# A token tower on one core: the score stacks of batch 0 turned on TensorE from token-major parts, x of batch 1 in other tiles, the next restack in two halves

## The reference

```python
h = onehot(x) @ embeddings                      # a gather of rows
q, k, v = split(layernorm(h) @ w_qkv)           # rotary embedding on q and k
attn = softmax(q @ k.T * hd ** -0.5)
h = h + (attn @ v) @ w_proj
y = layernorm(h)
e = argmax(y @ gate_w.T)                        # one of 8 experts for each token
out = h + y + y @ expert_w[e].T
```

## Time and profile before

| | |
|---|---|
| median of the runs | 322.32 us (320.94 to 324.34) |
| profiled execution | 324.0 us |
| its span, first to last instruction | 322.2 us |
| mean granted clock of TensorE | 0.944 |
| TensorE busy | 280.8 us, 87% |
| TensorE weight loads | 201.1 us, 62% |
| VectorE busy | 243.8 us, 76% |
| ScalarE busy | 127.0 us, 39% |
| GpSimd busy | 85.7 us, 27% |

### The profile page before, as it was taken

How to read it: one execution, slowest core, us unless ns; L and a number is a source line. 1 busy time by engine, 2 the same in 40 slices (tenths; PEclk the granted TensorE clock), 3 DMA queues, 4 the chain that set the end, 5 groups by cost and what they waited for, 6 DMA issues and landing times.

```text
span 322.2 us, 5465 instructions
## 1 busy us (share of the span) xinstructions
PE 280.8 (87%) x2000; PEld 201.1 (62%) x2000; DVE 243.8 (76%) x595; ACT 127.0 (39%) x261; POOL 85.7 (27%) x96
## 2 busy tenths in 40 slices
PE   0388489888878999989998999999999999999894
PEld 0267367454655777667765776676766766667582
DVE  6766667667798879887997799687988974657663
ACT  3032213643766543345343444353535435330100
POOL 4743500013567402250234113400210210210301
PEclk9999775558999999999999999999999999999998
DMA  4269492480191084015600470039000000001000
GB/s 115 73 247 149 66 161 28 83 119 1 25 161 27 9 142 58 4 36 113 91 6 32 92 117 4 0 94 139 4 33 4 1 28 10 3 1 35 0 33 33
DMA packets 11590, 19.14 MB, mean 59 GB/s; under 512 B 2012, under 2 KB 4903, under 8 KB 11436
## 3 DMA queue, kind: packets, MB, share of 16 engines
q1 hardware_dynamic: 10776, 18.23, 30.4%
q0 software_dynamic: 768, 0.55, 0.7%
q10 hardware_dynamic: 20, 0.02, 0.0%
HBM read 5.30 MB, written 2.10 MB: 23 GB/s over the span
## 4 chain that ended last, share of the span: by engine, by line
PE 47%; DVE 26%; issue 11%; POOL 5%; DMA 4%; ACT 4%; SPq 1%; POOLq 0%; DVEq 0%; ACTq 0%
PE e_bank L422 13%; PE o_bank L552 7%; DVE neg_max L863 7%; PE f_bank L422 7%; DVE acc L942 5%; PE t_pair L517 5%; DMA stacks<-parts 3%; PE s_pair L488 3%; POOL qk L342 2%; PE s_pair L422 2%; PE m_bank L564 2%; PE m_bank L422 2%; POOL res L360 2%; PE o_bank L422 1%; ACT parts L695 1%
## 5 line engine op out<-in xcount | busy, mean ns | idle before, releaser
L731 ACT ACTIVATE probs<-t_pair 128x512 f32<-128x512 f32 x128 | 69.7, 596 | 91.4 <-PE t_pair L517 91.0
L863 DVE TENSOR_REDUCE neg_max<-s_pair 128x2 f32<-128x512 f32 x128 | 82.0, 684 | 15.0 <-PE s_pair L488 15.0
L488 PE MATMUL s_pair<-stacks 48*128 48x256 f32 x256 | 54.8, 341 | 5.8 <-DVE neg_max L863 2.8
L517 PE MATMUL t_pair<-stacks 50*128 50x256 f32 x256 | 50.0, 325 | 2.0 <-DVE neg_max L863 1.7
L517 PEld LDWEIGHTS t_pair<-stacks 50*128 50x128 f32 x256 | 35.5, 199 | 24.4 <-issue 21.4
L422 PE MATMUL e_bank<-ew_h,y_h 128*128 128x512 f32 x92 | 40.3, 439 | 4.6 <-DVE acc L938 2.7
L488 PEld LDWEIGHTS s_pair<-stacks 48*128 48x128 f32 x256 | 38.9, 209 | 8.8 <-DVE neg_max L863 5.0
L552 PE MATMUL o_bank<-probs,vals 128*32 128x256 f32 x512 | 36.4, 405 | 1.2 <-ACT max_rows L695 1.2
L942 DVE SCALAR_TENSOR_TENSOR acc<-e_bank,mask,acc 128x256 f32<-128x256 f32 x66 | 28.9, 479 | 11.2 <-PE e_bank L422 11.2
L422 PE MATMUL e_bank<-ew_h,y_l 128*128 128x512 f32 x92 | 36.3, 395 | 0.0
L422 PE MATMUL e_bank<-ew_l,y_h 128*128 128x512 f32 x92 | 36.3, 395 | 0.0
(11 more groups left out here) (132 smaller groups left out, 532.1 us busy)
## 6 DMA issues: line engine op xcount, KB each, us to landing
stacks<-parts SPq DMA_DIRECT2D x48, 256.0 KB, 7.0
ew_raw<-in_expert_w SPq DMA_DIRECT2D x1, 2048.0 KB, 8.2
out<-res SPq DMA_DIRECT2D x8, 256.0 KB, 2.1
probs<-in_w_qkv SPq DMA_DIRECT2D x2, 384.0 KB, 3.8
stacks<-max_rows SPq DMA_DIRECT2D x30, 8.0 KB
h<-in_emb,ids POOLq DMA_INDIRECT x16, 2.6
probs<-in_w_proj SPq DMA_DIRECT2D x1, 256.0 KB, 2.6
stacks<-ones SPq DMA_DIRECT2D x6, 16.0 KB
```

The source lines that it names most:

```text
L488: m = mm(s_pair[:, half, t * N:(t + 1) * N], stacks[b % STACKS][r:r + KS, pair, 0, t * P:(t + 1) * P], stacks[b % STACKS][r:r + KS, pair, ...
L517: m = mm(t_pair[:, half, c * N:(c + 1) * N], stacks[b % STACKS][r:r + KM, pair, 1, c * P:(c + 1) * P], stacks[b % STACKS][r:r + KM, pair, ...
L731: nc.scalar.activation(probs[:, (2 * v + half) % RING, :, :].rearrange("p c n -> p (c n)"), t_pair[:, half, :], ACT.Exp, scale=SCALE).then ...
L863: v.tensor_reduce(neg_max[:, k // 4, :, 4 * half + k % 4], s_pair[:, half, :].rearrange("p (t n) -> p t n", t=NT), AX.X, ALU.max, negate=T ...
```

## The change

The stack of batch 0 is no longer made by transfers. The rotated q and k of batch 0, tokens by features, are split while they are still token-major: ScalarE copies high parts (`z_high`), GpSimd repeats one (`again_k`), VectorE subtracts (`z_low`), all into `zs`, which is the memory of stack 2 and has the order of a stack's rows along its free dimension, with ones where the last rows are. 32 transposes of 128x128 (`z_transpose`) turn it into eight PSUM banks, and ScalarE copies these into stack 0 (`z_copy`).

Since `qk` is used token-major by batch 0, `qk_high`, `qk_low` and `restack` begin with batch 1. x of batch 1 goes to the tiles `y_h[0]`, `y_l[0]`, so its copy needn't wait for v of batch 0. The restack of batch 1 is issued as twelve transfers, first six for heads 0 to 7, then six for the rest, each with its own semaphore. The prologues of all engines are reordered, and visits of stage -1 stand between them. v and both rotations of batch 2 move to slots 5, 0 and 1 of stage 0, its transposes to slots 2 and 3. The low part of w_proj is made on GpSimd and not on VectorE. The constants of `zs` are made early on VectorE, and both low parts of w_qkv stand ahead of batch 0's statistics.

The diff, cut to what is spoken of:

```diff
+        TWO = dict(rotate0=0, rotate1=1, t0=2, low0=3, t1=3, low1=4, v=5)
         POST = dict(o0=2, o1=4, norm0=3, norm1=5, on=6, o_low=7, proj=8, residual=9, stats=10, g_norm=11,
                     y=12, y_low=13, gate=14, gate_t=15, choose=15)
         LAST = dict(o0=2, o1=2, norm0=3, norm1=3, on=4, o_low=5, proj=6, residual=7, stats=7, g_norm=8,
...
         def v_bank(k):
-            return o_bank if k < 3 else f_bank
+            return o_bank if k < 2 else f_bank
+
+        def x_parts(k):
+            return (y_h[0], y_l[0]) if k == 1 else (x_h, x_l)
+
+        Z_BANKS = [[m_bank, o_bank, f_bank, e_bank], [s_bank[0], s_bank[1], t_bank[1], m_bank]]
+        Z_ORDER = [(0, 0), (0, 1), (1, 0), (1, 1), (1, 2), (0, 2), (0, 3), (1, 3)]
+
+        def z_copied(t, q):
+
+            return Z_ORDER.index((t, q)) + 1
+
+        def z_part(t, k, s):
+
+            return zs[:, :, k, t * P:(t + 1) * P].rearrange("p j (i r) -> p i j r", i=2)[:, :, :, s * HD:(s + 1) * HD]
+
+        def z_from(t, k):
+
+            return qk[:, t, 2 * k:2 * k + 2, :, :].rearrange("p i d j -> p i j d")
 
...
 
+            def first_restack():
+
+                sp.wait_ge(qkh_ok, NT)
+                for u in range(2):
+                    for i in range(3):
+                        if i == 1 and u == 0:
+                            sp.wait_ge(again_ok, NT)
+                            sp.wait_ge(qkl_ok, NT)
+                        for half in range(2):
+                            r = 64 * half
+                            sp.dma_start(
+                                stacks[1][r + i:r + KS:3, 4 * u:4 * u + 4, :, :].bitcast(F32).rearrange("d j k n -> d j (k n)"),
+                                parts[64 * u:64 * u + 64, half, 2 * i:2 * i + 2, :].bitcast(F32)).then_inc(half_in[u], 16)
...
-                ones_rows(i)
-            restack(0)
+            ones_rows(1)
+            sp.wait_ge(zt_ps, 8)
+            ones_rows(2)
+            first_restack()
             steps(step)
             sp.wait_ge(out_ok, 16 * (NB + 1))
...
+            def proj_weights_low():
+                pool.wait_ge(wp_h_ok, 1)
+                g.tensor_tensor(wp_l[:, :, :], wp_raw, wp_h[:, :, :].bitcast(F32), ALU.subtract).then_inc(wp_l_ok, 1)
+
+            def again_k(t):
+                wait(pool, rotated, t + 1)
+                g.tensor_copy(z_part(t, 1, 1), z_from(t, 1)).then_inc(z_dup_k, 1)
...
+            again_k(0)
             rotated_sum(0, 1)
+            again_k(1)
             f_rs_of(2)
             rotated_sum(1, 0)
             rotated_sum(1, 1)
-            gate_weights()
-            rotated_sum(2, 0)
-            rotated_sum(2, 1)
             steps(step)
 
 
...
             def project_v(b):
-                if b >= 3:
-                    wait(pe, qkl_ok, b * NT + NT)
+                if b >= 2:
+                    wait(pe, qkl_ok, (b - 1) * NT + NT)
+                elif b == 1:
+                    wait(pe, v_ok, b)
                 else:
-                    wait(pe, v_ok, b)
+                    pe.wait_ge(z_in, z_copied(0, 1))
+                x_h, x_l = x_parts(b)
...
+            def z_transpose(t):
+                wait(pe, z_unit, 1)
+                wait(pe, z_lo, 2 * t + 2)
+                wait(pe, z_dup_q, t + 1)
+                wait(pe, z_dup_k, t + 1)
+                if t == 0:
+                    wait(pe, xl_ok, 2)
+                    wait(pe, roped, 2 * NT)
+                for q in range(4):
+                    if t == 1 and q == 2:
+                        wait(pe, roped, 2 * NT + 2)
+                    if t == 1 and q == 3:
+                        wait(pe, z_in, z_copied(0, 0))
+                    for n in range(4):
+                        m = tr(Z_BANKS[t][q][:, n * P:(n + 1) * P].bitcast(F32R),
+                               zs[:, 2 * q + n // 2, n % 2, t * P:(t + 1) * P], ident_r[:, :])
+                    m.then_inc(zt_ps, 1)
+
             def scores_wait(b, v, half):
-                if v == 0:
-                    wait(pe, stack_in, b * 96 + 96)
+                if b == 0 and v == 0:
+                    wait(pe, z_in, z_copied(1, 1))
+                elif b == 0 and v in (4, 6):
+                    wait(pe, z_in, max(z_copied(0, v // 2), z_copied(1, v // 2)))
+                elif b == 1 and v % 4 == 0:
+                    wait(pe, half_in[v // 4], 96)
+                elif v == 0:
+                    wait(pe, stack_in, (b - 2) * 96 + 96)
                 wait(pe, max_ok, b * NH + 2 * v - half)
...
             pe.wait_ge(ident_ok, 1)
             x_transpose(0)
             project_qk(0, 0)
+            x_transpose(1)
             project_qk(0, 1)
+            project_qk(1, 0)
+            pe.wait_ge(identr_ok, 1)
+            z_transpose(0)
+            z_transpose(1)
+            visit(-1, 0)
+            project_qk(1, 1)
+            visit(-1, 1)
             project_v(0)
-            x_transpose(1)
-            qk_transpose(0, 0)
-            qk_transpose(0, 1)
-            project_qk(1, 0)
-            project_qk(1, 1)
+            visit(-1, 2)
+            qk_transpose(1, 0)
+            qk_transpose(1, 1)
+            visit(-1, 3)
             project_v(1)
             x_transpose(2)
-            qk_transpose(1, 0)
+            max_transpose(0, 0)
+            visit(-1, 4)
             project_qk(2, 0)
-            qk_transpose(1, 1)
+            visit(-1, 5)
             project_qk(2, 1)
-            pe.wait_ge(identr_ok, 1)
+            visit(-1, 6)
+            visit(-1, 7)
             steps(step)
 
 
...
             def x_high(b):
                 wait(act, xt_ps, b + 1)
-                wait(act, v_ps, b)
-                copy(x_h[:, :, :, :].rearrange("p c t n -> p (c t n)"), x_bank(b)[:, :]).then_inc(xh_ok, 1)
+                wait(act, v_ps, 1 if b == 2 else 0 if b == 1 else b)
+                copy(x_parts(b)[0][:, :, :, :].rearrange("p c t n -> p (c t n)"), x_bank(b)[:, :]).then_inc(xh_ok, 1)
...
+            def z_high(t):
+                wait(act, rotated, t + 1)
+                for k in range(2):
+                    copy(z_part(t, k, 0), z_from(t, k)).then_inc(z_hi, 1)
+                copy(z_part(t, 0, 2), z_from(t, 0)).then_inc(z_dup_q, 1)
+
+            def z_copy(t, q):
+                wait(act, zt_ps, 4 * t + q + 1)
+                copy(stacks[0][:, 2 * q:2 * q + 2, :, t * P:(t + 1) * P].rearrange("p j k n -> p (j k) n"),
+                     Z_BANKS[t][q][:, :].rearrange("p (m n) -> p m n", m=4)).then_inc(z_in, 1)
 
...
                 copy(wqkv_h[:, c, :], wqkv_raw[:, c, :]).then_inc(wqkv_h_ok, 1)
             x_high(0)
-            values(0)
-            qk_high(0, 0)
-            x_high(1)
-            qk_high(0, 1)
-            qk_high_again(0, 0)
-            qk_high_again(0, 1)
-            values(1)
-            x_high(2)
+            act.wait_ge(gw_in, 16)
+            copy(gw_parts[:, :, 0, :], gw_raw[:, :, :]).then_inc(gw_h_ok, 1)
             act.wait_ge(wp_in, 16)
             copy(wp_h[:, :, :], wp_raw).then_inc(wp_h_ok, 1)
-            act.wait_ge(gw_in, 16)
-            copy(gw_parts[:, :, 0, :], gw_raw[:, :, :]).then_inc(gw_h_ok, 1)
+            x_high(1)
+            z_high(0)
+            z_high(1)
+            for t, q in Z_ORDER:
+                z_copy(t, q)
+            values(0)
+            qk_high(1, 0)
+            qk_high(1, 1)
+            qk_high_again(1, 0)
+            qk_high_again(1, 1)
+            values(1)
+            max_row(0, 0)
+            x_high(2)
             steps(step)
 
 
...
+            def z_low(t):
+                for k in range(2):
+                    wait(dve, z_hi, 2 * t + k + 1)
+                    v.tensor_tensor(z_part(t, k, 1 + k), z_from(t, k), z_part(t, k, 0).bitcast(F32),
+                                    ALU.subtract).then_inc(z_lo, 1)
...
             v.memset(ones[:, :], 1.0).then_inc(ones_ok, 1)
+            v.memset(unit[:, :], 1.0).then_inc(filled, 1)
+            dve.wait_ge(filled, 1)
+            v.tensor_copy(zs[:, :, :, :].rearrange("p j k (t i r) -> p (j k t i) r", t=NT, i=2)[:, :, KS:],
+                          unit[:, :].rearrange("p (o r) -> p o r", o=1).broadcast_to([P, 64, HD])).then_inc(z_unit, 1)
+            qkv_weights_low()
             f_norm_a(0)
-            qkv_weights_low()
             f_norm_b(0)
             dve.wait_ge(ident_ok, 1)
             v.tensor_copy(ident_r[:, :], ident[:, :]).then_inc(identr_ok, 1)
+            f_norm_a(1)
+            x_low(0)
+            f_norm_b(1)
             for i in range(VALS):
                 v.memset(vals[i][:, :, :, HD:STRIP], 0.0).then_inc(h_zero, 1)
-            x_low(0)
-            f_norm_a(1)
-            f_norm_b(1)
             rotate(0, 0)
+            x_low(1)
+            f_norm_a(2)
             rotate(0, 1)
-            f_norm_a(2)
-            qk_low(0, 0)
-            x_low(1)
-            qk_low(0, 1)
+            z_low(0)
+            z_low(1)
+            rotate(1, 0)
             f_norm_b(2)
```

(38 more changed lines are left out.)

83 lines of the change are left out of this document (44 added, 39 removed).

## The result

The changed kernel takes 328.1 us (median, 327.6 to 329.3) against 323.1 for the kernel before in the same runs: a ratio of 1.0164, 95% interval 1.011 to 1.0218. It is slower by 1.6%. I had forecast 320.3 with a range to 326. The profiled execution took 327.57 us, span 325.8, against 324.0 and 322.2. It is the quickest of the four of the changed kernel, while the one profiled before stood 0.9 us above its median.

The account below looks back on a forecast made before the run. TensorE is busiest overall, but the gain was priced by the starts of the first two stages: 1.1 us from the fill and 0.9 from the first stage, 2.0 less, giving a median of 320.3 us, range 316 to 326.

Parts of the forecast that it names:

- The start of batch 0: Up to batch 0's first scores: without the wait for six transfers they come at 29.2, 7.6 us earlier than 36.79.
- the bound of 28.3: Early bound for batch 0's first scores: no hold between VectorE and GpSimd, transposes faster than the plain float kind.
- The hold between VectorE and GpSimd: Batch 0's start: a VectorE subtraction beside GpSimd's sum costs 0.35 us each way; bounds none, or 1.3 more.
- The power beside no low weights: Batch 0's statistics: GpSimd's power took 1.28 us beside the low weights and 0.72 alone, nearly cancelling VectorE's added work.
- The stall behind ScalarE's issues: Fill: VectorE stands 3.6 us before x_low of batch 2, whose copy waits behind ScalarE's two transfer issues.
- So I count one qk product at the lower clock: Fill's end: one slow qk product adds 1.2 us after overlap, moving the first stage's start from 49.9 to 51.1.
- The rival of a fall in the turning: Clock falls while batch 0's stacks are turned: first stage at 53.4, taking 24.5; 322.9 us, chance 0.20.
- So 12.6 plus 11.6, which is 24.2: First stage: fourth visit after 12.6 us, then 11.6 at the higher clock; 24.2 against 25.1, 0.9 gained.
- Behind 77.27 neither the order of work nor the clock changes: From the second stage's start at 77.27 on, everything is priced at zero.
- The rest at zero: y tiles cost nothing; restack halves nothing or 1 us; low output weights on GpSimd hidden, 0 to 0.5 if late.
- From the profile to the median: Whole kernel: the profiled execution stood 1.7 above the median of 322.3, so a forecast 322.0 becomes 320.3.
- the case of a clock that stays low: Rival for fill and first stage: stage starts at 54.9 and takes 28.9, 6.5 us slower; 328.8 us, chance 0.17.

Follow-up runs that it names:

- e1: Changed kernel with ScalarE copying x of batch 2 ahead of the row of maxima and its two transfer issues; 324.7 us, ratio 1.0055.
- e2: Changed kernel with v of batch 2 made in the fill, not in the first stage; 326.2 us, ratio 1.0119.
- e3: Changed kernel with added matmuls whose result nobody reads, in the fill and first stage; 323.4 us, ratio 1.0014.
- e7: e6 with VectorE's start reordered: x_low of batch 0, second rotation of batch 0 earlier, zeroing of value tiles later; 319.9 us, ratio 0.9905.
- e9: e7 with x of batch 2 prepared earlier, its qk products one visit earlier, four added matmuls left out; 318.9 us, ratio 0.9892.
- e10: e9 without the added matmuls whose result nobody reads; 321.0 us, ratio 0.9938.
- e8: Changed kernel with the restack of batch 1 in one piece, all landed before the first stage's first visit; 328.1 us, ratio 1.0148.
- e6: e5 with added matmuls whose result nobody reads, in the fill and first stage; 320.4 us, ratio 0.9936.
- e4: Kernel before the change with added matmuls whose result nobody reads, in the restack wait, fill and first stage; 322.9 us, ratio 0.9993.
- e5: Changed kernel with both edits of e1 and e2; 322.3 us, ratio 0.9991.

## Why the prediction was wrong, point by point

- *The start of batch 0*: right in kind. 28.05 against 29.2, outside the bound of 28.3 by 0.25. The whole difference stands ahead of GpSimd's sum for the second tile: batch 2's statistics didn't wait for their gather, they began at 19.87 and not 21.18, so the second rotation ended at 22.0 and not 23.45. Behind it two terms were off against each other: ScalarE's three copies of 128x256 took 1.88 us, not 1.1, and four of the transposes took 0.51 and followed each other at 0.34, not 0.45. (I had the pace of 128x256 copies from PSUM, 0.39. These go from SBUF to SBUF, with rows apart, while a plain copy of twice their size between SBUF tiles took 0.61; what slows them isn't shown.) The hold between VectorE and GpSimd came: two subtractions took 2.08 us across GpSimd's sum. The power beside no low weights took 0.73, as forecast.
- *The stall behind ScalarE's issues*: right in place and size, 4.0 us of VectorE against 3.6. e1 shows what it cost, 3.5 us, with 1.9 us of VectorE's idle time still left there.
- *"So I count one qk product at the lower clock"*: the first step that failed. The fill took 25.4 us from the first score to the first stage, not the 21.9 of the sum; 3.5 more, of which the earlier first score hides 1.1 in the stage's start (53.5 and not 51.1). Three products were slow: that of batch 1 from 28.8 (its six matmuls 0.43 apart) and both of batch 2, the last but for three matmuls. Ahead of the split of the maxima this is 1.8 us (12.1 and not 10.35), where I had counted nothing; behind x_low the two of batch 2 lie on the chain of waits with 2.9 and 2.3 us, 2.0 over the full clock, where I had 1.2, and that stretch took 1.3 more in all. The stall was 0.4 longer. The rival of a fall in the turning had the stage's start right (53.4), though from a first score at 30 that came at 28.05. By the rule of the Trainium skill that it was weighed with (TensorE: Matmul & The Clock Gate, Part 4) the transposes wouldn't hold the clock, and in the changed kernel's profile it went from 1.00 to 0.50 while they filled TensorE for 3.64 of 4 us from 24 to 28. But in five of the eleven profiles that turn the stacks this way the clock stayed at 1.00 through them (e2, e3, e7, e9, e10), behind as much idle time. So this case doesn't bear the rule out: the transposes alone don't settle what the clock does there.
- *"So 12.6 plus 11.6, which is 24.2"*: the second. The fourth visit came 13.2 us into the stage, close to 12.6. The clock did rise behind the v product and the outputs, near 67 us as I said. But it fell again near 71, and the rest took 13.9 us, not 11.6. In all the stage took 27.1 us (53.48 to 80.55), and 29.7 and 29.8 from split to split in the executions profiled in e1 and e8, against 27.9 here. I had 3.8 for v and its waits; the profiles put v at 1.4 to 3.2 at the lower clock (the changed kernel and e1, less e2) and 2.5 at a higher one (e3 at 0.93 less e6 at 1.00), and the medians at about 2. That term was rather too large than too small. Against it I had set 4.7 for a clock that would rise and stay up, and 2.3 of that came in this profile: that credit was the mistake.
- *"Behind 77.27 neither the order of work nor the clock changes"*: wrong by 0.6 here, and by 1.6 in e4. The clock falls in the second stage in some executions, too: it took 26.3 us at 1.00 before, 26.9 at 0.94 after, 27.9 at 0.94 in e4. From the third stage on the two profiles differ by 0.3.
- *The rest at zero* (x in the y tiles, halves, low weights on GpSimd): e8 bears it out for the halves. The low weights' sum on GpSimd ended at 17.95, ahead of the sum that began at 19.23. For the y tiles nothing was tried alone.
- *From the profile to the median*: I took 1.7 us off, since the execution profiled before stood that much above the median of three. The changed kernel's profile stands 0.6 below its median. So 5.6 of the 7.8 us between 320.3 and 328.1 are the steps above and what followed them, and 2.3 come from this one; part of it is which executions were profiled.
- *The chances*: the case of a clock that stays low had 0.17 and was left outside the range, though the one profile that I had showed just that from 47.5 to 74.4. Its sum, 328.8, is 0.7 from the 328.1 measured, and that is luck. It puts the first stage at 54.9 and its length at 28.9, and a profiled execution at 330.5, 2.9 above the measured one; and its clock didn't come: the granted one was 0.77 over the fill and 0.70 over the first stage, with four falls and as many rises. But a case between it and the forecast, with the clock falling and rising several times in fill and first stage, should have had the largest chance. The rows showed a stage of 26.90 us at 0.50 with TensorE busy for 23.88, and with a v product of 2.9 us more in it the clock was up only from about 67 to 71 and from 74 on.

So the loss is two things: the order around ScalarE's two issues (e1), and v of batch 2 ahead of the fourth visit (e5 against e1). Without both it is gone (e5). Each takes time itself, and the lower clock stretches what stands around it. The y tiles were not tried alone, but with them in place e5 has no loss left. What stays open is why a TensorE busy for 21.2 us of a stage has its full clock in e6 and 0.66 in e5: the added matmuls fill gaps, but which of their properties counts no run here tells. Nor does one tell why the clock falls in the turning of the stacks in some executions and not in others.

## What to carry to other kernels

Where a long wait is taken out, ask what the freed stretch will be filled with and in which order each queue takes it: here 8.7 us were won at the first score, and an issue of two transfers ahead of one copy gave back 3.5 of them. An engine that issues transfers is held by them (1.9 us for two here), so put whatever feeds another engine ahead. And price TensorE's work in a stretch at the clock that the profile grants there, not at the one that the change would need, with both levels in the range: one profile shows where the clock fell in one execution.

## What the runs showed that I had not expected

- Work that nobody reads can shorten a stage. With 21 matmuls of 128x512 added between the visits of the first stage and two ahead of it, the stage went from 26.4 to 23.4 us (e10, e9), and TensorE's busy time from 22.29 to 21.16. The medians differ by 2.1 us.
- The kernel before didn't profit from the same (e4): 2.3 us won at the second stage were 0.7 at the third, and the median moved by nothing. A gain of the clock in one stretch isn't a gain of the kernel until later stretches are looked at.
- Where the clock falls differs between executions of one kernel. The stacks of batch 0 are turned alike in eleven profiles, and the clock fell there in six of them. Among the executions of the kernel before that ran beside e1 to e4, the four quickest (320.1 to 320.6 us) had a mean granted clock of 0.958 to 0.965, and all from 322.3 us up had 0.936 to 0.948. So a part of the spread goes with the clock; another part does not, for executions with 0.941 lie from 322.3 to 324.3.
